# A linear attention's normaliser, as four column-grouped row products and one turning matmul per head

## The chip, the cores and the metric

The program runs on one NeuronCore of a Trainium2 chip. The metric is the device time of one execution in microseconds. The five engines that matter are TensorE (PE, whose weight loads appear apart as PEld), VectorE (DVE), ScalarE (ACT), GpSimd (POOL) and the DMA queues that SyncE (SP) issues. Each executes its own instructions in the order in which they were written, and they meet only through semaphores.

## The reference, cut to what matters

The program computes two layers. The change lies in the second layer's attention, which has 16 query heads of 128 channels, 4 key and value heads, 4 batches of 512 tokens and no softmax. For each batch:

```python
sq, sk = elu(q) + 1, elu(k) + 1                 # q: 16 heads, k: 4 heads, each [512, 128]
kv    = einsum('bhsd,bhse->bhde', sk, v)
qkv   = einsum('bhsd,bhde->bhse', sq, kv)
k_sum = sk.sum(axis=2)
norm  = einsum('bhsd,bhd->bhs', sq, k_sum)      # the normaliser: one number per token and head
attn  = qkv / (norm[..., None] + 1e-6)
out   = attn @ Wo.T                             # heads side by side, 2048 channels to 512
```

The kernel folds the last product into the heads: for head h it makes M = kv @ Wo_h (128 x 512), then sq_h @ M, scaled row by row by 1/norm and added into one accumulator `acc`.

## The kernel before, in words

The program is a sequence of stages: `front`, `recurrence_and_gate`, `linear_attention`, `relu_gate`. Only `linear_attention` changes. It works batch by batch (b = 0 to 3; the first has a few extra steps for loading and splitting the weights). In a batch TensorE turns the normalised input (`xT`), projects k and v for four tiles of 128 tokens each, makes `kvT` and `ksum`, and then goes through the 16 heads. All of its work is a list of jobs, `jobs`, which is the order in which TensorE issues them. `Ring` hands each job the next of the 8 PSUM banks, so job number i may start only when the reader of job i - 8 has finished (`ring.vacated`).

In the part with the heads the list reads, for each h: `q h`, `M h`, `norm h-1`, `head h-1` for the four token tiles. Head h's query product thus runs ahead of head h-1's output products. What each job is on TensorE:

- `q h`: 12 products of 128x512, the three-term split of an exact float32 product into pairs of fp32r (function `product3`, lines 579 to 581), four input tiles deep.
- `M h`: one float32 product of 128x512 (L1725). The trace has two records for each float32 product.
- `norm h`: four float32 products (L1730), one per token tile. The stationary operand is a tile of `sq` (128x128), the moving operand one column, the key sum `ksum`. The result is 128 tokens x 1 for each tile, which is the shape VectorE needs: tokens on partitions.
- `head h, t`: three products of 128x512, one of the four output tiles.

What surrounds the heads on the other engines, per head and in this order:

- ScalarE: `reluq` (relu of q, L1660), `expq` (exp of VectorE's min, L1664), the high part of M (`M_part[0]`, L1669). Ahead of `expq` it waits for VectorE's min of the same head, and VectorE waits for `reluq`.
- VectorE: min(q, 0) (L1571), in some heads a step of the next batch's layer norm (L1517 to L1532), then norm + 1e-6 (L1582) and its reciprocal (L1587), four accumulations into `acc` (L1598), the low part of M (L1606), and `sq` split into its two parts (L1611, L1613).
- GpSimd: `sq` = `expq` + `reluq` (L1495).

Of the kernel before, what the change touches and what calls it, by code (L numbers as in the profile page):

```python
# [14 lines left out]
P = 128  # L15
B = 4
T = 512
TT = T // P
# [1275 lines left out]
def linear_attention(nc, w, x1, spill, relay, handed, hand):  # L1294
# [11 lines left out]
    for h in range(QH + 1):  # L1306
        if h < QH:
            jobs += [("q", h), ("M", h)]
        if h > 0:
            jobs += [("norm", h - 1)] + [("head", h - 1, t) for t in range(TT)]  # L1310

    with ExitStack() as ctx:
# [25 lines left out]
        kvT = sb("kvT", [P, KVH, D])  # L1338
        ksum = sb("ksum", [P, KVH])
        expq = [sb(f"expq{i}", [P, T]) for i in range(2)]  # L1340
# [39 lines left out]
        sq_hi_ready = signal("sq_hi_ready", QH)  # L1380
        sq_lo_ready = signal("sq_lo_ready", QH)
        norm_ready = signal("norm_ready", QH)
        inv_ready = signal("inv_ready", QH)
# [10 lines left out]
        for h in range(QH):  # L1394

            reader["q", h] = (minq_ready, h + 1)
            reader["M", h] = (M_lo_ready, h + 1)
            reader["norm", h] = (norm_ready, h + 1)
            for t in range(TT):
                reader["head", h, t] = (acc_ready, h * TT + t + 1)  # L1400
# [64 lines left out]
        def _(pool):  # L1465
# [16 lines left out]
            def sequence(b, first, last):  # L1482
                for h in range(QH):
                    if first and h + AHEAD < QH:
                        low(h + AHEAD)
                    if h == (LN_HEAD if first else RSQRT_HEAD) and not last:
# [5 lines left out]

                    pool.wait_ge(*(ring.product(("norm", h - 2), b) if h >= 2 else
                                   ring.product_before(("norm", QH - 2 + h), b)))
                    nc.gpsimd.tensor_tensor(sq[h % 2][:, :], expq[h % 2][:, :], reluq[h % 2][:, :],  # L1495
# [129 lines left out]
        def _(act):  # L1625
            for s in (xT_ready, expk_ready, kvT_ready, ksum_ready, reluq_ready, expq_ready, M_hi_ready):
                s.ahead(act)

            def high(h):
# [5 lines left out]
            def sequence(b, first):  # L1635
# [14 lines left out]
                act.wait_ge(*ring.product(("ksum", 0), b))  # L1650
                nc.scalar.activation(ksum[:, :], ring.place(("ksum", 0))[:, 0:KVH], ACT.Copy).then_inc(ksum_ready.sem, 1)

                act.wait_ge(w_loaded, 3 * 16)
                act.wait_ge(*sk_ready.now(b, TT))
                for h in range(QH):
                    if first and h + AHEAD < QH:
# [6 lines left out]
                    act.wait_ge(*minq_ready.now(b, h + 1))  # L1663
                    nc.scalar.activation(expq[h % 2][:, :], expq[h % 2][:, :], ACT.Exp).then_inc(expq_ready.sem, 1)  # L1664
                    act.wait_ge(*ring.product(("M", h), b))

                    act.wait_ge(*(ring.product(("head", h - 2, TT - 1), b) if h >= 2 else
                                  ring.product_before(("head", QH - 2 + h, TT - 1), b)))
                    nc.scalar.activation(M_part[h % 2][0][:, :], ring.place(("M", h))[:, :],  # L1669
                                         ACT.Copy).then_inc(M_hi_ready.sem, 1)  # L1670

            sequence(0, True)
# [4 lines left out]
        def _(pe):  # L1677
# [4 lines left out]
            def sequence(b, first):  # L1682
                for job in jobs:
# [37 lines left out]
                    elif kind == "M":  # L1721
# [3 lines left out]
                        last = nc.tensor.matmul(place[:, :], kvT[:, n // GROUPS, :], Wo[:, n, :], start=True, stop=True)  # L1725
                    elif kind == "norm":
                        pe.wait_ge(*sq_ready.now(b, n + 1))
                        pe.wait_ge(*ksum_ready.now(b, 1))
                        for t in range(TT):
                            last = nc.tensor.matmul(place[:, t:t + 1], sq[n % 2][:, t * P:(t + 1) * P],  # L1730
                                                    ksum[:, n // GROUPS:n // GROUPS + 1], start=True, stop=True)
                    else:
                        t = job[2]
                        pe.wait_ge(*M_lo_ready.now(b, n + 1))
                        pe.wait_ge(*sq_lo_ready.now(b, n + 1))
                        last = product3(nc, place[:, :], [q[:, t * P:(t + 1) * P] for q in sq_part[n % 2]],
                                        [q[:, :] for q in M_part[n % 2]], True, True)
# [533 lines left out]
```

## Time and profile before

| | us |
|---|---|
| median of 3 runs | 1979.46 (1970.95 to 1991.2) |
| profiled execution | 1981.94 |
| its span, first to last instruction | 1980.1 |
| TensorE busy in it | 1805.2 (91%), mean granted clock 0.953 |
| VectorE busy | 1204.3 (61%) |
| ScalarE busy | 369.7 (19%) |
| GpSimd busy | 549.2 (28%) |
| span of the stage `linear_attention`, about | 890 to 1540 |

A profile comes from one execution. Its rows give a start in us from the first instruction, a duration, the engine, the line of the kernel, the operation, what it writes and reads, and how often. The durations of matmuls are modelled ends over measured starts: matmuls overlap, so that the distance between two starts, not the duration, is what one costs TensorE. A granted clock of 1.00 is 2.4 GHz, 0.50 is 1.2 GHz.

### The profile page before, as it was taken

The numbers are of one execution on the slowest core, as the hardware profiler recorded it, in microseconds if no ns is written. First come the engines' busy times: TensorE is split into PE (matmuls) and PEld (weight loads), VectorE is DVE, ScalarE is ACT, GpSimd is POOL, SyncE is SP. The second block draws the span as 40 slices with busy tenths as digits, with TensorE's granted clock in tenths as the row PEclk, the third lists the DMA queues.
The fourth block names the chain that finished last, engine by engine and source line by source line (L and its number), as shares of the span: only waits on it lengthen the run. The fifth ranks groups of instructions, "written<-read, shape, count | busy, mean of one in ns | idle before, by whom it ended". The sixth has DMA issues, their size and how long they took to land. (4 is left out here: it accounts for less than half of the span.)

```text
span 1980.1 us, 22000 instructions
## 1 busy us (share of the span) xinstructions
PE 1805.2 (91%) x6900; PEld 1187.2 (60%) x6900; DVE 1204.3 (61%) x1821; ACT 369.7 (19%) x621; POOL 549.2 (28%) x419
## 2 busy tenths in 40 slices
PE   7898894898998989939998999999999699999997
PEld 3333333655646647416775876777677356788885
DVE  4776784676877768633775686577477554523333
ACT  1212221011011111102331222122122221211111
POOL 3443442344553554331320121111011232101001
PEclk9999996898999989968999999999999799999998
DMA  4423328663675745403101001001100221302010
GB/s 188 180 96 133 140 102 272 220 220 116 199 223 180 223 162 199 142 33 144 38 33 64 1 1 64 0 0 51 55 0 0 75 74 32 139 1 85 5 58 32
DMA packets 81236, 197.06 MB, mean 100 GB/s; under 512 B 6352, under 2 KB 28752, under 8 KB 72592
## 3 DMA queue, kind: packets, MB, share of 16 engines
q1 hardware_dynamic: 81168, 196.27, 29.1%
q8 instruction: 28, 0.46, 0.1%
q14 instruction: 40, 0.33, 0.1%
HBM read 152.21 MB, written 44.04 MB: 99 GB/s over the span
## 5 line engine op out<-in xcount | busy, mean ns | idle before, releaser
L846 POOL TENSOR_TENSOR r_rS<-r_S,r_rT 128x512 f32<-128x512 f32 x128 | 182.9, 1430 | 259.4 <-DVE r_S L935 259.4
L1495 POOL TENSOR_TENSOR l_sq<-l_expq,l_reluq 128x512 f32<-128x512 f32 x64 | 83.1, 1299 | 474.9 <-ACT l_expq L1664 474.9
L1598 DVE SCALAR_TENSOR_TENSOR l_acc<-l_ps,l_inv,l_acc 128x512 f32<-128x512 f32 x240 | 167.0, 749 | 29.6 <-PE l_ps L581 29.6
L579 PE MATMUL r_ps<-relay_part,r_w_part 128*128 128x512 f32 x352 | 149.5, 425 | 21.9 <-DMA r_w_part<-scratch_wgu 13.5
L935 DVE TENSOR_TENSOR_SCAN r_S<-r_dT,r_ps 128x512 f32<-128x512 f32 x128 | 156.3, 1221 | 11.4 <-POOL r_rS L846 7.1
L1265 PE MATMUL r_ps<-Wdn,r_h 128*128 128x512 f32 x352 | 154.9, 596 | 0.0
L1991 DVE CAST g_x_part<-g_x 128x512 fp32r<-128x512 f32 x64 | 37.6, 587 | 187.6 <-ACT g_x L2049 187.6
L581 PE MATMUL r_ps<-relay_part,r_w_part 128*128 128x512 f32 x352 | 142.4, 405 | 0.0
L580 PE MATMUL r_ps<-relay_part,r_w_part 128*128 128x512 f32 x352 | 142.2, 404 | 0.0
L1265 PEld LDWEIGHTS r_ps<-Wdn,r_h 128*128 128x128 f32 x352 | 65.6, 190 | 86.6 <-issue 86.6
L579 PE MATMUL l_ps<-l_M_part,l_sq_part 128*128 128x512 f32 x256 | 107.4, 420 | 8.0 <-DVE l_sq_part L1613 8.0
L1698 PE MATMUL l_ps<-relay,l_xT 128*128 128x512 f32 x256 | 111.1, 594 | 0.0
L1571 DVE TENSOR_SCALAR l_expq<-l_ps,l_bq 128x512 f32<-128x512 f32 x64 | 48.0, 750 | 97.4 <-ACT l_reluq L1660 97.4
L579 PE MATMUL l_ps<-l_x_part,l_Wq 128*128 128x512 f32 x256 | 106.4, 416 | 0.0
L579 PE MATMUL g_ps<-g_x_part,g_Wup 128*128 128x512 f32 x256 | 104.2, 407 | 1.6 <-DVE g_x_part L1979 1.6
L581 PE MATMUL l_ps<-l_x_part,l_Wq 128*128 128x512 f32 x256 | 104.4, 408 | 0.0
L579 PE MATMUL g_ps<-g_Wdn,g_x_part 128*128 128x512 f32 x256 | 104.2, 407 | 0.0
L580 PE MATMUL l_ps<-l_x_part,l_Wq 128*128 128x512 f32 x256 | 104.0, 406 | 0.0
L581 PE MATMUL g_ps<-g_x_part,g_Wup 128*128 128x512 f32 x256 | 102.7, 401 | 0.0
L580 PE MATMUL g_ps<-g_x_part,g_Wup 128*128 128x512 f32 x256 | 102.6, 401 | 0.0
L580 PE MATMUL l_ps<-l_M_part,l_sq_part 128*128 128x512 f32 x256 | 101.8, 398 | 0.0
L581 PE MATMUL l_ps<-l_M_part,l_sq_part 128*128 128x512 f32 x256 | 101.4, 396 | 0.0
(184 smaller groups left out, 3422.3 us busy)
## 6 DMA issues: line engine op xcount, KB each, us to landing
r_w_part<-scratch_wgu SPq DMA_DIRECT2D x44, 1024.0 KB, 5.2
r_V<-scratch_v SPq DMA_DIRECT2D x96, 256.0 KB
scratch_wgu<-f_halves SPq DMA_DIRECT2D x32, 384.0 KB, 3.6
relay<-scratch_x SPq DMA_DIRECT2D x12, 1024.0 KB, 6.7
relay<-scratch_v SPq DMA_DIRECT2D x32, 256.0 KB
relay<-in_x SPq DMA_DIRECT2D x4, 1024.0 KB, 9.0
scratch_x<-f_xT SPq DMA_DIRECT2D x4, 1024.0 KB, 8.7
r_xs<-in_x SPq DMA_DIRECT2D x4, 1024.0 KB, 6.8
```

Of the source, the lines that this page charges most:

```text
L579: nc.tensor.matmul(out, left[1], right[0], start=start, stop=False)
L580: nc.tensor.matmul(out, left[0], right[1], start=False, stop=False)
L581: return nc.tensor.matmul(out, left[0], right[0], start=False, stop=stop)
L846: nc.gpsimd.tensor_tensor(rS[u % RS][:, :], S[u % 2][:, 0:T], rT[u // DK][:, :], ALU.mult).then_inc(rS_ready.sem, 1)
L935: nc.vector.tensor_tensor_scan(S[u % 2][:, 1:T + 1], dT[hh][:, :], kv, 0.0, ALU.mult, ALU.add).then_inc(S_ready.sem, 1)
L1265: last = nc.tensor.matmul(place[0][:, :], h[:, j, n * P:(n + 1) * P], Wdn[:, j, :], start=(j == 0), stop=(j == JT - 1))
L1495: nc.gpsimd.tensor_tensor(sq[h % 2][:, :], expq[h % 2][:, :], reluq[h % 2][:, :], ALU.add).then_inc(sq_ready.sem, 1)
L1571: nc.vector.tensor_scalar(expq[h % 2][:, :], ring.place(("q", h))[:, :], bq[:, h:h + 1], 0.0, ALU.add, ALU.min).then_inc(minq_ready.sem, 1)
L1598: last = nc.vector.scalar_tensor_tensor(acc[:, t, :], ps, inv[g % 2][:, t:t + 1], acc[:, t, :], ALU.mult, ALU.add)
L1698: last = nc.tensor.matmul(place[:, :], xT[:, kt, n * P:(n + 1) * P], Wkv[kind][:, kt, :], start=(kt == 0), stop=(kt == KT - 1))
L1991: nc.vector.tensor_copy(hi[:, :], x2[j % 2][:, :]).then_inc(x2_hi_ready.sem, 1)
```

## The change

Per head the job `norm` is split in two. The new job `rows` multiplies the other way round: the stationary operand is `ksum`, copied out to 32 equal columns, and the moving operand is a 128-token tile of `sq` (128x128). Each of the four tiles goes to its own group of 32 columns of the array, so its result lands on 32 partitions of the bank, and the four together fill 128 partitions x 128: 32 equal rows for each token tile. ScalarE copies this block to SBUF (`copy_rows`, tile `norm_rows`), and the new job `norm` is one float32 product with `norm_rows` stationary and four columns of the identity moving, which gives the 128 tokens x 4 that VectorE read before. VectorE's work is unchanged.

The job list becomes, for each h: `q h`, `rows h-1`, `M h`, `head h-1, 0`, `norm h-1`, `head h-1, 1` to `3`. It is 8 jobs per head, where it was 7. On ScalarE `copy_rows(h-1)` stands behind `expq` of head h and ahead of the high part of M. `ksum` grows from 128x4 to 128x4x32, written by the same ScalarE instruction, once per batch.

```diff
--- before.py
+++ after.py
@@ -1305,9 +1305,13 @@
             + [("kvT", 0), ("ksum", 0)])
     for h in range(QH + 1):
         if h < QH:
-            jobs += [("q", h), ("M", h)]
+            jobs += [("q", h)]
         if h > 0:
-            jobs += [("norm", h - 1)] + [("head", h - 1, t) for t in range(TT)]
+            jobs += [("rows", h - 1)]
+        if h < QH:
+            jobs += [("M", h)]
+        if h > 0:
+            jobs += [("head", h - 1, 0), ("norm", h - 1)] + [("head", h - 1, t) for t in range(1, TT)]
 
     with ExitStack() as ctx:
         def sb(name, shape, dt=F32):
@@ -1336,7 +1340,8 @@
         sk = sb("sk", [P, TT, KVH * D])
         v = sb("v", [P, TT, KVH * D])
         kvT = sb("kvT", [P, KVH, D])
-        ksum = sb("ksum", [P, KVH])
+        ksum = sb("ksum", [P, KVH, P // TT])
+        norm_rows = [sb(f"norm_rows{i}", [P, P]) for i in range(2)]
         expq = [sb(f"expq{i}", [P, T]) for i in range(2)]
         reluq = [sb(f"reluq{i}", [P, T]) for i in range(2)]
         biased, expk = reluq, expq
@@ -1379,6 +1384,7 @@
         x_lo_ready = signal("x_lo_ready", KT)
         sq_hi_ready = signal("sq_hi_ready", QH)
         sq_lo_ready = signal("sq_lo_ready", QH)
+        rows_ready = signal("rows_ready", QH)
         norm_ready = signal("norm_ready", QH)
         inv_ready = signal("inv_ready", QH)
         acc_ready = signal("acc_ready", QH * TT)
@@ -1395,6 +1401,7 @@
 
             reader["q", h] = (minq_ready, h + 1)
             reader["M", h] = (M_lo_ready, h + 1)
+            reader["rows", h] = (rows_ready, h + 1)
             reader["norm", h] = (norm_ready, h + 1)
             for t in range(TT):
                 reader["head", h, t] = (acc_ready, h * TT + t + 1)
@@ -1490,8 +1497,8 @@
 
                     pool.wait_ge(*(sq_lo_ready.now(b, h - 1) if h >= 2 else sq_lo_ready.before(b, QH - 1 + h)))
 
-                    pool.wait_ge(*(ring.product(("norm", h - 2), b) if h >= 2 else
-                                   ring.product_before(("norm", QH - 2 + h), b)))
+                    pool.wait_ge(*(ring.product(("rows", h - 2), b) if h >= 2 else
+                                   ring.product_before(("rows", QH - 2 + h), b)))
                     nc.gpsimd.tensor_tensor(sq[h % 2][:, :], expq[h % 2][:, :], reluq[h % 2][:, :],
                                             ALU.add).then_inc(sq_ready.sem, 1)
 
@@ -1623,8 +1630,15 @@
 
         @block.scalar
         def _(act):
-            for s in (xT_ready, expk_ready, kvT_ready, ksum_ready, reluq_ready, expq_ready, M_hi_ready):
+            for s in (xT_ready, expk_ready, kvT_ready, ksum_ready, reluq_ready, expq_ready, rows_ready, M_hi_ready):
                 s.ahead(act)
+
+            def copy_rows(b, h):
+                act.wait_ge(*ring.product(("rows", h), b))
+                act.wait_ge(*(ring.product(("norm", h - 2), b) if h >= 2 else
+                              ring.product_before(("norm", QH - 2 + h), b)))
+                nc.scalar.activation(norm_rows[h % 2][:, :], ring.place(("rows", h))[:, 0:P],
+                                     ACT.Copy).then_inc(rows_ready.sem, 1)
 
             def high(h):
                 cols = slice(h * D, (h + 1) * D)
@@ -1648,7 +1662,8 @@
                 act.wait_ge(*ring.product(("kvT", 0), b))
                 nc.scalar.activation(flat(kvT[:, :, :]), ring.place(("kvT", 0))[:, :], ACT.Copy).then_inc(kvT_ready.sem, 1)
                 act.wait_ge(*ring.product(("ksum", 0), b))
-                nc.scalar.activation(ksum[:, :], ring.place(("ksum", 0))[:, 0:KVH], ACT.Copy).then_inc(ksum_ready.sem, 1)
+                nc.scalar.activation(ksum[:, :, :], ring.place(("ksum", 0))[:, 0:KVH].unsqueeze(2).broadcast_to(
+                    [P, KVH, P // TT]), ACT.Copy).then_inc(ksum_ready.sem, 1)
 
                 act.wait_ge(w_loaded, 3 * 16)
                 act.wait_ge(*sk_ready.now(b, TT))
@@ -1662,12 +1677,15 @@
 
                     act.wait_ge(*minq_ready.now(b, h + 1))
                     nc.scalar.activation(expq[h % 2][:, :], expq[h % 2][:, :], ACT.Exp).then_inc(expq_ready.sem, 1)
+                    if h > 0:
+                        copy_rows(b, h - 1)
                     act.wait_ge(*ring.product(("M", h), b))
 
                     act.wait_ge(*(ring.product(("head", h - 2, TT - 1), b) if h >= 2 else
                                   ring.product_before(("head", QH - 2 + h, TT - 1), b)))
                     nc.scalar.activation(M_part[h % 2][0][:, :], ring.place(("M", h))[:, :],
                                          ACT.Copy).then_inc(M_hi_ready.sem, 1)
+                copy_rows(b, QH - 1)
 
             sequence(0, True)
             with act.Fori(1, B) as b:
@@ -1723,12 +1741,17 @@
                         if first and n == 0:
                             pe.wait_ge(wo_loaded, 16)
                         last = nc.tensor.matmul(place[:, :], kvT[:, n // GROUPS, :], Wo[:, n, :], start=True, stop=True)
-                    elif kind == "norm":
+                    elif kind == "rows":
                         pe.wait_ge(*sq_ready.now(b, n + 1))
                         pe.wait_ge(*ksum_ready.now(b, 1))
+                        width = P // TT
                         for t in range(TT):
-                            last = nc.tensor.matmul(place[:, t:t + 1], sq[n % 2][:, t * P:(t + 1) * P],
-                                                    ksum[:, n // GROUPS:n // GROUPS + 1], start=True, stop=True)
+                            last = nc.tensor.matmul(place[t * width:(t + 1) * width, 0:P], ksum[:, n // GROUPS, :],
+                                                    sq[n % 2][:, t * P:(t + 1) * P], start=True, stop=True)
+                    elif kind == "norm":
+                        pe.wait_ge(*rows_ready.now(b, n + 1))
+                        last = nc.tensor.matmul(place[:, 0:TT], norm_rows[n % 2][:, :], ident[:, 0:P:P // TT],
+                                                start=True, stop=True)
                     else:
                         t = job[2]
                         pe.wait_ge(*M_lo_ready.now(b, n + 1))
```

TensorE in the heads of a middle batch, before: the end of the job `q`, then `M` (L1725), `norm` (L1730), and the first of the next heads' tiles (`l_M_part`, `l_sq_part`); `l_ps5` and so on are the PSUM banks.

```order
L581 MATMUL l_ps5<-l_x_part0,l_Wq0 128x512
L1686 REGISTER_ALU
L1725 MATMUL l_ps6<-l_Wo,l_kvT 128x512
L1730 MATMUL l_ps7<-l_ksum,l_sq1 128x1 x4
L579 MATMUL l_ps0<-l_M_part01,l_sq_part11 128x512
L580 MATMUL l_ps0<-l_M_part11,l_sq_part01 128x512
L581 MATMUL l_ps0<-l_M_part01,l_sq_part01 128x512
L1686 REGISTER_ALU
L579 MATMUL l_ps1<-l_M_part01,l_sq_part11 128x512
```

The same place after the change:

```order
L581 MATMUL l_ps0<-l_x_part0,l_Wq0 128x512
L1749 MATMUL l_ps1<-l_sq1,l_ksum 32x128 x4
L1743 MATMUL l_ps2<-l_Wo,l_kvT 128x512
L1704 REGISTER_ALU
L579 MATMUL l_ps3<-l_M_part01,l_sq_part11 128x512
L580 MATMUL l_ps3<-l_M_part11,l_sq_part01 128x512
L581 MATMUL l_ps3<-l_M_part01,l_sq_part01 128x512
L1753 MATMUL l_ps4<-l_ident,l_norm_rows1 128x4
L1704 REGISTER_ALU
L579 MATMUL l_ps5<-l_M_part01,l_sq_part11 128x512
```

The four row products stand ahead of M, and the product that turns them stands between the head's first and second tile.

ScalarE over one head in the same place, before: relu, exp and the high part of M.

```order
L1660 ACTIVATE l_reluq1<-l_ps0,l_bq 128x512 [waits l_sq_ready,l_product]
L1663 REGISTER_ALU
L1664 ACTIVATE l_expq1<-l_expq1 128x512 [waits l_minq_ready]
L1665 REGISTER_ALU
L1667 REGISTER_ALU [waits l_product]
L1669 ACTIVATE l_M_part01<-l_ps1 128x512 [waits l_product]
```

And after:

```order
L1675 ACTIVATE l_reluq0<-l_ps0,l_bq 128x512 [waits l_sq_ready,l_product]
L1678 REGISTER_ALU
L1679 ACTIVATE l_expq0<-l_expq0 128x512 [waits l_minq_ready]
L1637 REGISTER_ALU
L1638 REGISTER_ALU [waits l_product]
L1640 ACTIVATE l_norm_rows1<-l_ps1 128x128 [waits l_product]
L1682 REGISTER_ALU
L1684 REGISTER_ALU [waits l_product]
L1686 ACTIVATE l_M_part00<-l_ps2 128x512 [waits l_product]
```

The copy of head h-1's rows (`l_norm_rows1`) stands behind the exp of head h (`l_expq0`), which itself waits for VectorE's min of head h (`l_minq_ready`).

## Rows read from the trace of the kernel before

**Rows 1.** Windows: us, busy time (count) by engine, PEclk, DMA share, GB/s.
```profile
488.00:600.00 112.00, 105.17 (x391) 60.88 (x390) 83.07 (x102) 16.09 (x30) 60.78 (x41) 0.99 0.65 207
...
1115.00:1220.00 105.00, 103.11 (x490) 82.20 (x489) 83.77 (x160) 24.80 (x43) 19.15 (x15) 1.00 0.00 1
```
**Rows 2.** Timeline, PE, one head: start us, us, engine, line, op, out<-in, count.
```profile
1201.62 0.39 PE L581 MATMUL l_ps<-l_x_part,l_Wq 128*128 128x512 f32 x1
1201.86 1.02 PE L1725 MATMUL l_ps<-l_Wo,l_kvT 128*128 128x512 f32 x2
1202.71 0.95 PE L1730 MATMUL l_ps<-l_ksum,l_sq 128*128 128x1 f32 x8
1203.52 0.48 PE L579 MATMUL l_ps<-l_M_part,l_sq_part 128*128 128x512 f32 x1
1203.84 0.40 PE L580 MATMUL l_ps<-l_M_part,l_sq_part 128*128 128x512 f32 x1
...
1206.36 0.40 PE L579 MATMUL l_ps<-l_x_part,l_Wq 128*128 128x512 f32 x1
...
1209.15 1.02 PE L1725 MATMUL l_ps<-l_Wo,l_kvT 128*128 128x512 f32 x2
```
**Rows 3.** Timeline of ACT over the same head; in brackets the idle time before.
```profile
1202.06 0.69 ACT L1660 ACTIVATE l_reluq<-l_ps,l_bq 128x512 f32<-128x512 f32 x1 [4.68 <-PE l_ps L581]
1203.56 0.63 ACT L1664 ACTIVATE l_expq<-l_expq 128x512 f32<-128x512 f32 x1 [0.82 <-DVE l_expq L1571]
1204.10 0.58 ACT L1669 ACTIVATE l_M_part<-l_ps 128x512 fp32r<-128x512 f32 x1
```
**Rows 4.** Timeline of DVE over the same head.
```profile
1202.78 0.75 DVE L1571 TENSOR_SCALAR l_expq<-l_ps,l_bq 128x512 f32<-128x512 f32 x1 [1.02 <-ACT l_reluq L1660]
...
1203.90 0.15 DVE L1582 TENSOR_SCALAR l_norm<-l_ps 128x4 f32<-128x4 f32 x1
1204.08 0.18 DVE L1587 RECIPROCAL l_inv<-l_norm 128x4 f32<-128x4 f32 x1
1204.59 2.81 DVE L1598 SCALAR_TENSOR_TENSOR l_acc<-l_ps,l_inv,l_acc 128x512 f32<-128x512 f32 x4 [0.32 <-PE l_ps L581]
...
1208.36 0.69 DVE L1613 TENSOR_TENSOR l_sq_part<-l_sq,l_sq_part 128x512 fp32r<-128x512 f32 x1
```
**Rows 5.** Lines of ACT by form: busy us, mean ns, idle before.
```profile
L1669 ACT ACTIVATE l_M_part<-l_ps 128x512 fp32r<-128x512 f32 x64 | 37.2, 581 | 0.0
...
L1651 ACT ACTIVATE l_ksum<-l_ps 128x4 f32<-128x4 f32 x4 | 0.7, 174 | 14.4 <-PE l_ps L1711 14.4
```
**Rows 6.** Timeline of PE around a column-grouped product in the recurrence stage.
```profile
490.77 0.40 PE L581 MATMUL r_ps<-relay_part,r_w_part 128*128 128x512 f32 x1
491.10 1.07 PE L1237 MATMUL r_ps<-r_rS,r_pick 128*32 128x512 f32 x8
492.10 1.09 PE L1182 MATMUL r_ps<-r_ident,r_o 128*128 128x128 f32 x8
493.38 0.50 PE L579 MATMUL r_ps<-relay_part,r_w_part 128*128 128x512 f32 x1 [0.19 <-DVE r_h L946]
```
**Rows 7.** Timeline of the weight loads (PEld) there.
```profile
491.10 0.16 PEld L1237 LDWEIGHTS r_ps<-r_rS,r_pick 128*32 128x32 f32 x8 [0.37 <-issue]
```
**Rows 8.** Timeline of PE at the end of batch 1.
```profile
1216.49 0.47 PE L579 MATMUL l_ps<-l_M_part,l_sq_part 128*128 128x512 f32 x1 [1.90 <-DVE l_sq_part L1613]
...
1219.30 1.91 PE L1690 MATMUL l_ps<-l_ident,relay 128*128 128x128 f32 x16
```
**Rows 9.** Timeline of DVE there.
```profile
1215.65 0.69 DVE L1613 TENSOR_TENSOR l_sq_part<-l_sq,l_sq_part 128x512 fp32r<-128x512 f32 x1
```
**Rows 10.** Timeline of PE near the end of batch 0.
```profile
1047.59 1.20 PE L1730 MATMUL l_ps<-l_ksum,l_sq 128*128 128x1 f32 x8 [4.06 <-DVE l_M_part L1606]
...
1049.31 0.63 PE L580 MATMUL l_ps<-l_M_part,l_sq_part 128*128 128x512 f32 x1
1049.73 0.63 PE L581 MATMUL l_ps<-l_M_part,l_sq_part 128*128 128x512 f32 x1
```

## The prediction, made before the changed kernel ran

> **What bounds the kernel now.** I read the page first (TensorE busy 91% of the span), then the windows, then one head in the timelines. In the middle of a batch of this stage TensorE is busy 103.11 of 105 us at a granted clock of 1.00, VectorE 83.77, ScalarE 24.80 [rows 1]. The timeline of TensorE shows a closed pattern: M starts at 1201.86 and again at 1209.15, so one head takes 7.29 us, and no row in between has idle time [rows 2]. TensorE alone sets the time there. The reader should see in the same rows what follows what: the last query product starts at 1201.62, M takes 0.85 (1201.86 to 1202.71), the normaliser 0.81 (to 1203.52), the head's twelve products run from 1203.52 to 1206.36, then the next query.
>
> ScalarE is idle for most of a head, but what it does comes in a fixed chain behind the query product [rows 3, 4]: relu at 1202.06, VectorE's min at 1202.78, exp at 1203.56, and the copy of M at 1204.10. The last starts 2.48 us after the last query product began. Today nobody on TensorE waits for the end of this chain in the same head. After the change somebody does, and this is what I cost below.
>
> **The change, part by part.**
>
> Removed: the four normaliser products, 0.81 us per head, and with them the slow start of the product behind them, whose second record comes 0.32 after the first, where 0.23 is usual [rows 2]: 0.09. Together 0.90.
>
> Added, the row products. This trace has the same form in the recurrence stage: four products of 32 columns each, two records each, 512 elements moving [rows 6]. The eight records hold TensorE from 491.10 to 492.10, 1.00 us. A single float32 product of 512 elements costs 0.85 [rows 2], 0.43 per record, so the four column groups run side by side: two record times, not eight. With 128 elements moving, each record time is a quarter, 0.11 in place of 0.43: 1.00 - 2 x 0.32 = 0.36. Entering costs 0.33 from start to start in place of 0.23 [rows 6], and the load of the weights stood idle for 0.37 ahead of it [rows 7]: 0.10 more. M behind it cannot have its weights loaded ahead either; the product at 493.38 with such a start took 0.50 in place of 0.40 [rows 6]: 0.10 more. Together 0.56.
>
> Added, the turning product: one of the four of today, 0.81 / 4 = 0.20, with the 0.09 behind it.
>
> If nobody waited, a head would change by -0.90 + 0.56 + 0.29 = -0.05 us, over 64 heads -3 us. That is not the forecast, because of the wait.
>
> Added, the wait. The turning product reads `norm_rows`, ScalarE writes that in `copy_rows(h-1)`, and this stands behind exp of head h. So it cannot start before the place where the copy of M starts now, 1204.10 in the head shown [rows 3]. Neither the row products nor their speed matters for it; they are done over a microsecond earlier. The copy is 128x128: between 0.174 us for 4 elements and 0.581 for 512 [rows 5], straight between them 0.27. Its release of TensorE I put at 0.10, between 0.03 (VectorE's min ends at 1203.53, exp starts at 1203.56 [rows 3, 4]) and 0.15 (the split ends at 1216.34 [rows 9], TensorE starts at 1216.49 [rows 8]). So the turning product starts at 1204.10 + 0.27 + 0.10 = 1204.47.
>
> When would TensorE be there? Row products at 1201.62 + 0.33 = 1201.95, M at 1202.31, the head's first tile at 1202.31 + 0.10 + 0.85 = 1203.26, three products of 0.23: 1203.95. It stands idle for 0.5 us in each head.
>
> From 1204.47 the path goes on: the turning product 0.20, its weights not loaded ahead 0.10, then nine products of the head, 0.32 + 8 x 0.23 = 2.16. The next query starts at 1206.93, today at 1206.36 [rows 2]: **+0.57 us per head**. It is a closed loop, query, relu, min, exp, copy, turn, three tiles, next query, so every head pays it.
>
> The Trainium skill (ScalarE: Activation LUTs, Rules for kernel authors) budgets about 0.3 us per activation plus 0.83 ns per element, an estimate of 0.41 for this copy. The rows do not agree: 0.581 for 512 elements, where it would give 0.72 [rows 5]. By the page the sum would be about 8 us higher.
>
> The same skill (TensorE: Matmul & The Clock Gate, Step-by-step: what each phase is for) says that the next weights load while the current matmul runs. Here the weights are what is waited for, and the row at 493.38 shows the load in the open after a wait [rows 6]. By the page alone, 0.10 less per head, the sum would be 6 us lower.
>
> Which heads pay: in each batch the turning products of heads 0 to 14 stand behind an exp, 15 x 4 = 60. One falls into the stall at the end of batch 0, where VectorE's layer norm holds TensorE for 4.06 us and the clock is at 1.2 GHz for some products behind it [rows 10]; I count nothing there. 59 x 0.57 = 33.6 us.
>
> The end of a batch: head 15 already waits for VectorE (1.90 us idle [rows 8]), with no query product to cover it. VectorE now reads the normaliser later: the turning product from 1204.47 and about 0.4 for its length and end, 1204.9, and another 0.4 for its two short operations, so the accumulation starts at about 1205.3 in place of 1204.59 [rows 4], 0.7 later. The last head starts that much later and has the turning product (0.29) within it, where today the normaliser lay in the idle time: +1.0 x 4 = 4 us.
>
> At nothing: VectorE's delay of 0.7 elsewhere. Its split of `sq` ends at 1209.05 [rows 4], and the next head's first product, which needs it, starts one period behind 1203.52 [rows 2], at 1210.81: 1.8 us of room. The copy of M comes 0.27 later; VectorE takes it up only behind four accumulations, over 3 us later [rows 3, 4]. The wider `ksum` is written once per batch, ahead of the query products. With eight jobs per head and eight banks each job waits for the reader of its own kind one head earlier, and all of these end before; the tightest is M's, whose reader has over 1 us. If VectorE's cover were gone, its delay would be added one for one.
>
> Sum: 33.6 + 4 = +37.6 us, on the profiled execution's 1981.94. That execution was 2.5 above the median of 1979.46, so against the median I say **2016 us**.
>
> Bounds: shortest of everything (copy 0.17, release 0.03, no open load) gives 1206.66, +0.30 per head and +20 us in all. Longest (copy as long as a full one, 0.58, release 0.15) gives 1207.29, +0.93 and +60. A copy of a quarter of the elements is nearer to 0.174 than to 0.581, so I take the straight line and the upper end is unlikely.
>
> **The rivals.**
>
> (a) The wait does not decide: the copy is there when TensorE arrives, at 1203.95. Then only TensorE's own sum counts, -3 us, about 1976. The point is 1204.47 against 1203.95: the chain would have to be 0.5 us shorter than rows 3 and 4 show. For it speaks that matmul ends are modelled; against it that starts are measured and ScalarE issues in order. A share of this case, with M also starting at once and the turning product almost free, would end faster by at most 0.2 x 64 = 13 us. 7%.
>
> (b) The clock: with 0.5 us of idle time in each 7.9, TensorE could fall to 1.2 GHz in parts. At the end of batch 0 it did behind 4.06 us of idle time, with starts 0.42 apart in place of 0.23 [rows 10]. Against it: in the recurrence stage TensorE was busy 105.17 of 112, 94%, at a clock of 0.99 [rows 1], and here it would be busy 94% too. If a tenth of the 470 us of heads ran at half the clock, +47 us more (64 x 7.3 / 10), 2063. 6%.
>
> (c) The column groups do not run side by side at 128 elements: eight records of 0.11 instead of two, +0.5 us. TensorE would arrive at 1204.45, still ahead of 1204.47. 2017: the same forecast; it changes what the profile shows, not the time. I put 10% on it, inside the forecast's share.
>
> (d) The chain is shorter by 0.2 to 0.4 us, by the lower bounds: 1990 to 2000. 10%.
>
> The forecast, (c) within it, has 77%.
>
> **Numbers.** The three runs of before spread over 20 us, so 1% (20 us) is about what can be told from no change. Faster by over 1%: part of (a), 2%. Within 1%: the rest of (a), 5%, and most of (d), 6%: 11%. Slower: 87%. The range from 1996 to 2034 leaves out (a), (b) and the lower edge of (d).
>
> **What would show it.** In the profile after: TensorE's turning product idle for about 0.5 us before it, released by ScalarE's copy, some 60 times; the copy at about 0.27 us, right behind exp; M starting every 7.86 us; the eight row records within 0.3 us of each other. The forecast is wrong if M comes every 7.3 us, if no idle time stands before the turning product, or if PEclk in these windows falls below 0.95.

## The result, and the profile after

| | before | after |
|---|---|---|
| median | 1978.28 us (4 runs) | 2012.88 us (4 runs, 2012.39 to 2015.07) |
| ratio to before | | 1.0164, 95% interval 1.0117 to 1.021 |
| profiled execution, its span | 1981.94, 1980.1 | 2015.07, 2013.2 |
| TensorE busy, granted clock | 1805.2 us (91%), 0.953 | 1813.4 us (90%), 0.953 |

The change made the kernel 1.6% slower, 34.6 us in the median and 33.1 between the two profiled executions. The prediction said 2016.

The timeline of TensorE over a head in the middle of the stage (start us, us, engine, line, operation), which answers to [rows 2]:

```profile
1209.87 0.70 PE L1743 MATMUL l_ps<-l_Wo,l_kvT 128*128 128x512 f32 x1
...
1217.02 0.39 PE L581 MATMUL l_ps<-l_x_part,l_Wq 128*128 128x512 f32 x1
...
1217.34 0.42 PE L1749 MATMUL l_ps<-l_sq,l_ksum 128*32 128x128 f32 x8
1217.69 1.13 PE L1743 MATMUL l_ps<-l_Wo,l_kvT 128*128 128x512 f32 x2
...
1218.88 0.39 PE L580 MATMUL l_ps<-l_M_part,l_sq_part 128*128 128x512 f32 x1
1219.11 0.40 PE L581 MATMUL l_ps<-l_M_part,l_sq_part 128*128 128x512 f32 x1
1219.89 0.36 PE L1753 MATMUL l_ps<-l_ident,l_norm_rows 128*128 128x4 f32 x2 [0.38 <-ACT l_norm_rows L1640]
1220.13 0.47 PE L579 MATMUL l_ps<-l_M_part,l_sq_part 128*128 128x512 f32 x1
```

M starts at 1209.87 and at 1217.69: a head takes 7.82 us, where it took 7.30. All four row products with their eight records stand between 1217.34 and 1217.69. Then comes the new hole. The head's third product starts at 1219.11, the next could start 0.23 later, at 1219.34, and the turning product (L1753) starts at 1219.89, 0.55 us later. The row gives the idle time as 0.38, since it counts from the modelled end of the product before, and it names who ended it: ScalarE's copy.

ScalarE over the same head, which answers to [rows 3]:

```profile
1217.44 0.69 ACT L1675 ACTIVATE l_reluq<-l_ps,l_bq 128x512 f32<-128x512 f32 x1 [5.03 <-PE l_ps L581]
1218.95 0.63 ACT L1679 ACTIVATE l_expq<-l_expq 128x512 f32<-128x512 f32 x1 [0.82 <-DVE l_expq L1578]
1219.49 0.26 ACT L1640 ACTIVATE l_norm_rows<-l_ps 128x128 f32<-128x128 f32 x1
1219.64 0.59 ACT L1686 ACTIVATE l_M_part<-l_ps 128x512 fp32r<-128x512 f32 x1
```

The copy starts where M's copy did, 2.47 us after the last query product's start (2.48 before), and ends at 1219.75. The row products that it reads had all begun before M did, at 1217.69. In the 0.82 us ahead of exp ScalarE had nothing to do.

The waits of the stage, in total, times and longest, tell the same for all heads:

```profile
PE l_ps L1753 <- ACT l_norm_rows L1640: 23.2, 59, 0.6
...
PE l_ps L579 <- DVE l_sq_part L1620: 10.9, 5, 2.6
```

59 heads wait for the copy, as counted beforehand. The second row is mostly the ends of the four batches. TensorE there, in batch 1, which answers to [rows 8]:

```profile
1225.40 0.50 PE L579 MATMUL l_ps<-l_M_part,l_sq_part 128*128 128x512 f32 x1 [2.61 <-DVE l_sq_part L1620]
...
1226.12 0.63 PE L581 MATMUL l_ps<-l_M_part,l_sq_part 128*128 128x512 f32 x1
1226.54 0.42 PE L1753 MATMUL l_ps<-l_ident,l_norm_rows 128*128 128x4 f32 x2
1226.82 0.77 PE L579 MATMUL l_ps<-l_M_part,l_sq_part 128*128 128x512 f32 x1
...
1227.82 0.63 PE L581 MATMUL l_ps<-l_M_part,l_sq_part 128*128 128x512 f32 x1
1228.25 0.63 PE L579 MATMUL l_ps<-l_M_part,l_sq_part 128*128 128x512 f32 x1
...
1230.05 1.91 PE L1708 MATMUL l_ps<-l_ident,relay 128*128 128x128 f32 x16
```

The last head starts 2.61 us of idle time late, and then its products follow each other at 0.43 us (1227.82 to 1228.25) where 0.23 is usual. The granted clock from 1226.10 to 1229.00 is 0.50, which is 1.2 GHz. Before, after 1.90 us of idle time, the twelve products took 2.81 us (1216.49 to 1219.30 [rows 8]) at a granted clock of 1.00; now they and the turning product take 4.65.

The window in the middle of the stage, which answers to [rows 1] (us, busy time by engine, PEclk, DMA share, GB/s):

```profile
1115.00:1220.00 105.00, 99.66 (x486) 67.84 (x484) 76.79 (x146) 27.37 (x56) 17.97 (x15) 1.00 0.00 1
```

TensorE lost 3.5 us of busy time in the window, and its clock stayed at 2.4 GHz.

### The profile page after: what moved, and what is told of

The parts are those of the page before. It is cut to its first block and busy times, and to the rows that moved or that the text cites. A ratio compares the mean times of both kernels' runs of the same rounds, so it can differ in the third digit from the quotient of the medians.

```text
span 2013.2 us, 22497 instructions
## 1 busy us (share of the span) xinstructions
PE 1813.4 (90%) x7028; PEld 1144.1 (57%) x7028; DVE 1204.4 (60%) x1821; ACT 381.0 (19%) x685; POOL 549.6 (27%) x419
## 5 line engine op out<-in xcount | busy, mean ns | idle before, releaser
L579 PE MATMUL l_ps<-l_M_part,l_sq_part 128*128 128x512 f32 x256 | 131.4, 513 | 10.9 <-DVE l_sq_part L1620 10.9
L579 PE MATMUL g_ps<-g_Wdn,g_x_part 128*128 128x512 f32 x256 | 104.7, 409 | 0.0
L581 PE MATMUL l_ps<-l_M_part,l_sq_part 128*128 128x512 f32 x256 | 103.5, 404 | 0.0
L580 PE MATMUL l_ps<-l_M_part,l_sq_part 128*128 128x512 f32 x256 | 102.8, 402 | 0.0
L581 PE MATMUL g_ps<-g_Wdn,g_x_part 128*128 128x512 f32 x256 | 102.1, 399 | 0.0
```

The lines of the kernel that those rows point to most:

```text
L579: nc.tensor.matmul(out, left[1], right[0], start=start, stop=False)
L580: nc.tensor.matmul(out, left[0], right[1], start=False, stop=False)
L581: return nc.tensor.matmul(out, left[0], right[0], start=False, stop=stop)
```

## Where the time went

For each kernel I took the starts of M from TensorE's timeline. "Heads" is the sum over the four batches from the first M to the sixteenth. "Ends" is the sum from the sixteenth M to the next batch's first product, so idle time at the turn of the loop over batches is in it; in the last batch it ends 0.23 us behind the start of the last head product. All are of the profiled executions. The first interval between two M's holds no head products (3.7 us before, 4.2 to 4.4 after), so that a batch has 14 full heads in "heads", and the output products of heads 14 and 15 are in "ends".

| kernel | a head | heads | ends | heads + ends |
|---|---|---|---|---|
| before | 7.30 | 424.2 | 49.0 | 473.2 |
| after | 7.82 | 461.3 | 49.6 | 510.9 |
| copy ahead of exp | 7.18 | 425.2 | 46.8 | 472.0 |
| rows twice | 7.82 | 462.2 | 47.1 | 509.3 |
| turn one tile later | 7.20 | 426.9 | 53.5 | 480.4 |
| copy behind M | 8.31 | 488.5 | 57.7 | 546.2 |
| copy ahead of exp, rows twice | 7.41 | 437.9 | 53.0 | 490.9 |
| copy ahead of exp, one column group | 7.83 | 462.0 | 46.1 | 508.1 |
| before, one product of four | 6.67 | 390.9 | 51.2 | 442.1 |
| copy ahead of exp, last turn first | 7.18 | 425.2 | 46.4 | 471.6 |
| the same, last split first | 7.18 | 425.3 | 42.7 | 468.0 |
| before, last split first | 7.30 | 424.2 | 40.5 | 464.7 |
| copy ahead of exp, last split first | 7.18 | 425.1 | 37.4 | 462.6 |

The stage's heads and ends grew by 37.7 us. The rest of the program, of which the change touches only the one `ksum` instruction per batch, was 4.6 us shorter in the profiled execution of after than of before.

The sums of "heads" hide a shift. In batch 0 the layer norm's stall lay behind the sixteenth M before (106.6 and 17.4 us) and lies ahead of it now (119.0 and 12.7), because with eight jobs per head M waits for the reader of the M before it. So batches 1 to 3 are the ones to compare: 105.9 became 114.2, and an end of 10.15 (1209.15 [rows 2] to 1219.30 [rows 8]) became 12.36 (1217.69 to 1230.05).

## The experiments

### The copy ahead of exp

```diff
                                          bias=bq[:, h:h + 1]).then_inc(reluq_ready.sem, 1)
+                    if h > 0:
+                        copy_rows(b, h - 1)
                     act.wait_ge(*minq_ready.now(b, h + 1))
                     nc.scalar.activation(expq[h % 2][:, :], ...Exp).then_inc(expq_ready.sem, 1)
-                    if h > 0:
-                        copy_rows(b, h - 1)
```

> The changed kernel with one move: on ScalarE the copy of head h-1's rows stands between relu and exp of head h, where ScalarE is idle for 0.82 us. Theory (the wait behind exp costs everything): the copy ends over a microsecond before TensorE reaches the turning product, the idle time of about 0.5 us before it goes, a head takes 7.25 us (7.82 less 0.55), and the time falls from 2013 to about 1977, within 5 us of the kernel before. Rival (the change costs by TensorE's own work: the switch to column groups and back, and one more product): nothing on TensorE changes, 2013 stays within 5.

Measured: 1977.68 us (12 runs), 0.999 of before, interval 0.997 to 1.0009. ScalarE and TensorE in one head:

```profile
1187.34 0.69 ACT L1675 ACTIVATE l_reluq<-l_ps,l_bq 128x512 f32<-128x512 f32 x1 [4.55 <-PE l_ps L581]
1187.92 0.27 ACT L1640 ACTIVATE l_norm_rows<-l_ps 128x128 f32<-128x128 f32 x1
1188.84 0.63 ACT L1681 ACTIVATE l_expq<-l_expq 128x512 f32<-128x512 f32 x1 [0.65 <-DVE l_expq L1578]
```

```profile
1187.59 1.13 PE L1743 MATMUL l_ps<-l_Wo,l_kvT 128*128 128x512 f32 x2
...
1189.01 0.40 PE L581 MATMUL l_ps<-l_M_part,l_sq_part 128*128 128x512 f32 x1
1189.24 0.28 PE L1753 MATMUL l_ps<-l_ident,l_norm_rows 128*128 128x4 f32 x2
1189.38 0.48 PE L579 MATMUL l_ps<-l_M_part,l_sq_part 128*128 128x512 f32 x1
...
1194.77 1.13 PE L1743 MATMUL l_ps<-l_Wo,l_kvT 128*128 128x512 f32 x2
```

The copy lies in what was idle time, the turning product follows 0.23 behind the product before it, and a head takes 7.18 us. Moving one ScalarE instruction by one place gives back 35 us, the whole of the loss. TensorE's own work, which is identical in both kernels, is thus not the cause. It is even 0.12 us per head cheaper than before. That does not reach the total, for heads and ends are only 1.2 us shorter than before: in batches 1 to 3 the heads fell from 317.6 to 314.7 us, and the ends grew from 31.7 to 34.9. TensorE at the end of batch 1 of this kernel:

```profile
1201.85 0.47 PE L579 MATMUL l_ps<-l_M_part,l_sq_part 128*128 128x512 f32 x1 [2.64 <-DVE l_sq_part L1620]
...
1203.88 0.63 PE L579 MATMUL l_ps<-l_M_part,l_sq_part 128*128 128x512 f32 x1
1204.30 0.63 PE L580 MATMUL l_ps<-l_M_part,l_sq_part 128*128 128x512 f32 x1
```

The last head waits for VectorE's split as before. TensorE merely comes there earlier and stands idle for 2.64 us instead of 1.90, and again products behind it are 0.42 apart.

### The row products twice

```diff
-                        for t in range(TT):
+                        for t in [*range(TT), *range(TT)]:
                             last = nc.tensor.matmul(place[t * width:(t + 1) * width, 0:P], ...
```

> The changed kernel with the four row products issued twice, the second time over the first. Theory: TensorE has 0.55 us of idle time ahead of the turning product, and the added work (eight more records, 0.2 to 0.36 us) fits in it: a head stays at 7.82, the time at 2013, at most 3 more. Rival (TensorE's own work sets the time): 60 x 0.2 to 0.36, 12 to 22 us more, 2025 to 2035.

Measured: 2015.05 us, 1.0181 of before (1.0153 to 1.021); after was 2012.88. A head takes 7.82 us as in the changed kernel, and its hole has shrunk:

```profile
1187.72 0.64 PE L1749 MATMUL l_ps<-l_sq,l_ksum 128*32 128x128 f32 x16
1188.29 1.13 PE L1743 MATMUL l_ps<-l_Wo,l_kvT 128*128 128x512 f32 x2
1190.27 0.36 PE L1753 MATMUL l_ps<-l_ident,l_norm_rows 128*128 128x4 f32 x2 [0.17 <-ACT l_norm_rows L1640]
```

The added 0.22 us (0.57 for the block instead of 0.35) came out of the idle time, 0.17 in place of 0.38. TensorE's work is off the path.

### The turning product one tile later

```diff
-            jobs += [("head", h - 1, 0), ("norm", h - 1)] + [("head", h - 1, t) for t in range(1, TT)]
+            jobs += ([("head", h - 1, 0), ("head", h - 1, 1), ("norm", h - 1)]
+                     + [("head", h - 1, t) for t in range(2, TT)])
```

> The changed kernel with the turning product one tile later in the job list, between the head's second and third tile. ScalarE's order is untouched. Theory: three more products (0.69 us) stand ahead of it, TensorE arrives 3.02 us after the start of the last query product where the rows are ready after 2.85, so the idle time goes and a head takes 7.25 to 7.35: about 1978. VectorE gets its normaliser 0.15 us later than in the changed kernel. Rival (TensorE's own work): 2013. If VectorE's later start mattered, it would be slower than 2013.

Measured: 1987.29 us (10 runs), 1.0043 of before (1.0019 to 1.0068). A head takes 7.20 us, as the theory has it: the wait is gone with ScalarE's order untouched. But the whole is 9 us slower than expected, and 10 slower than the kernel with the copy ahead of exp. The table shows where most of it is: the batch ends took 53.5 us instead of 46.8. TensorE at the end of batch 1:

```profile
1204.38 0.28 PE L1754 MATMUL l_ps<-l_ident,l_norm_rows 128*128 128x4 f32 x2
...
1209.81 0.77 PE L579 MATMUL l_ps<-l_M_part,l_sq_part 128*128 128x512 f32 x1 [3.33 <-DVE l_sq_part L1621]
```

The last head waits 3.33 us instead of 2.6. The turning product of head 14 starts 2.35 us behind M where it was 1.65 in the kernel with the copy ahead of exp, so VectorE gets the normaliser 0.7 us later, and at a batch's end nothing covers that. Four times 0.7 is 2.8 of the 6.7 us. The last head also starts at the low clock here: its first product lasts 0.77 us, 0.47 in the kernel with the copy ahead of exp.

### The copy behind the copy of M

```diff
-                    if h > 0:
-                        copy_rows(b, h - 1)
                     act.wait_ge(*ring.product(("M", h), b))
 ...
                     nc.scalar.activation(M_part[h % 2][0][:, :], ...Copy).then_inc(M_hi_ready.sem, 1)
+                    if h > 0:
+                        copy_rows(b, h - 1)
```

> The changed kernel with the copy of the rows one place later on ScalarE, behind the high part of M (about 0.5 us from start to start). Theory: the loop gets longer by all of it, 8.32 us per head in place of 7.82, 59 x 0.5 = 30 us more, 2043. Rival (TensorE's own work): no change, 2013.

Measured: 2056.96 us (2042.33 to 2059.2), 1.0373 of before (1.0333 to 1.0412). A head takes 8.31 us, 8.32 was expected, and heads and ends together are 35.3 us more than in the changed kernel. ScalarE and TensorE:

```profile
1207.52 0.58 ACT L1684 ACTIVATE l_M_part<-l_ps 128x512 fp32r<-128x512 f32 x1
1207.99 0.27 ACT L1640 ACTIVATE l_norm_rows<-l_ps 128x128 f32<-128x128 f32 x1
```

```profile
1208.40 0.35 PE L1753 MATMUL l_ps<-l_ident,l_norm_rows 128*128 128x4 f32 x2 [0.86 <-ACT l_norm_rows L1640]
```

Three places for one copy give 7.18, 7.82 and 8.31 us per head. From the second place to the third the copy starts about 0.47 us later, which is what M's copy ahead of it takes from start to start (1207.52 to 1207.99), and the head is 0.49 longer. In the first place nobody waits for it, and TensorE's own work sets the 7.18. The total is 44 us above after, 14 more than expected. Of these 5.3 are in heads and ends, in part the loop-end idle time told below; the rest lies outside them, and I did not settle it.

### The same doubling where nothing waits

The kernel with the copy ahead of exp, and the row products twice as above.

> The kernel with the copy between relu and exp, and the four row products issued twice. There the loop no longer has idle time, so the same added work that cost 2 us in the changed kernel should now be paid: theory: eight records more, 0.2 to 0.3 us per head on top of 7.18, 60 x 0.25 = 15 us, from 1978 to about 1993. Rival (small column-grouped products are hidden beside their neighbours whatever waits): 1978 stays.

Measured: 2000.91 us, 1.0105 of before (1.0065 to 1.0144). A head takes 7.41 instead of 7.18. The 0.23 that was free in the changed kernel is paid here in every head, 12.7 us over the heads. The ends took 6.2 us more, 2.6 of it idle time at the turns of the loop over batches, so the total is 23 above its base, not 15. Heads and ends account for 18.9 of the 23.

### All rows in one column group

```diff
-                            last = nc.tensor.matmul(place[t * width:(t + 1) * width, 0:P], ...
+                            last = nc.tensor.matmul(place[0:width, t * P:(t + 1) * P], ...
```

> The kernel with the copy between relu and exp, and all four row products written to the same 32 columns of the array, side by side along the bank (so the normaliser is made of other numbers; only the time is read). If the four column groups run side by side in the changed kernel, they cannot here: eight records of 0.11 in place of two, +0.5 us per head, 7.7, about 30 us more, 2008. If they did not run side by side anyway: 1978.

Measured: 2016.3 us, 1.0183 of before (1.0144 to 1.0222), 39 us above its base, 8 more than expected. The block of eight records:

```profile
1175.63 1.06 PE L1749 MATMUL l_ps<-l_sq,l_ksum 128*32 128x128 f32 x8
1176.62 0.70 PE L1743 MATMUL l_ps<-l_Wo,l_kvT 128*128 128x512 f32 x1
```

0.99 us from start to start, where the four groups take 0.35, and 7.83 us per head, 0.65 more; 60 times that is the 39. The column groups do run side by side at 128 elements; without it the change would lose 0.5 us per head against before even with the copy in the better place.

### One normaliser product of four, in the kernel before

```diff
-                        for t in range(TT):
+                        for t in range(1):
                             last = nc.tensor.matmul(place[:, t:t + 1], sq[n % 2][:, t * P:(t + 1) * P],
```

> The kernel before the change with one of its four normaliser products per head (the other three columns of the normaliser are left out; only the time is read). It measures what such a product costs TensorE in place: by the rows, 0.81 / 4 = 0.20 us each, three less are 0.61 per head, a head at 6.69 in place of 7.30, 60 x 0.61 = 37 us less, 1943. If the first of them carried most of the price (the weights that cannot be loaded ahead), less than 20 us would go: 1960 or more.

Measured: 1948.94 us, 0.9807 of before (0.9759 to 0.9855). A head takes 6.67 in place of 7.30: 0.21 per product, 0.20 was the term of the sum. Heads and ends are 31.1 us less, not 37. The heads gave 33.3, for an interval between two M's at the start of each batch hardly changed (7.25 in batches 1 and 2), and the ends grew by 2.2: the last head waits for VectorE there, so it started at nearly the same time behind M (7.15 us in batch 1, before 7.34), and in batch 1 seven of the eleven distances between its products were 0.42 or 0.43 us, where before all but the first were 0.22 or 0.23.

### The batch end

Three more kernels with the copy ahead of exp, and one without the change. First the turning product of head 15 ahead of that head's first tile:

```diff
-        if h > 0:
+        if 0 < h < QH:
             jobs += [("head", h - 1, 0), ("norm", h - 1)] + [("head", h - 1, t) for t in range(1, TT)]
+        if h == QH:
+            jobs += [("norm", h - 1)] + [("head", h - 1, t) for t in range(TT)]
```

> The kernel with the copy between relu and exp, and for the last head of a batch the turning product ahead of the head's first tile, so that it lies in the idle time in which TensorE waits for VectorE's split of head 15. Theory: 0.15 to 0.25 us per batch and VectorE's read of the normaliser a little earlier: 1 us in all, 1977. If the turning product at the end mattered more than by its own length: 1973.

Measured: 1978.09 us (12 runs), 0.9982 (0.996 to 1.0005): no difference from 1977.68 that these runs can tell.

Then, on top, VectorE's split of M and `sq` for head 15 ahead of the normaliser and accumulations of head 14 (`split(h)` is the block of L1606 to L1613):

```diff
+                    if h == QH - 1:
+                        split(h)
                     if h > 0:
                         g = h - 1
 ...
-                    if h < QH:
+                    if h < QH - 1:
+                        split(h)
```

> As the kernel before it, and on VectorE the split of M and of sq for head 15 ahead of the reading of the normaliser and the accumulations of head 14. Theory: the last head no longer waits for four accumulations and then the split, it starts about 6.4 us after the last query product's start in place of 7.9, TensorE's idle time there falls from 2.6 to about 1 us and the clock is not lowered behind it: 2 to 3 us per batch, 8 to 12 in all, 1967. Rival (the accumulations of head 14 only move the wait to the banks of head 15): 1977.

Measured: 1972.02 us (12 runs), 0.9949 of before (0.9926 to 0.9971), about half of the gain that was expected. The same move in the kernel before the change:

> The kernel before the change, with only VectorE's order at a batch's last head altered as in the kernel before this one: the split for head 15 ahead of the normaliser and accumulations of head 14. It tells how much of the 0.5% of that kernel comes from this move and how much from the change with its copy moved. Theory: all four batch ends lose the 1.9 us of TensorE's idle time; if TensorE then stands idle ahead of the next batch's first product as it did there (3.8 us, released by nothing that the profile shows), the gain is small, 0 to 4 us: 1976 to 1980, and the rest of the 0.5% is the change's. If the move alone gives all of it: 1971.

Measured: 1970.72 us (12 runs), 0.9948 (0.9925 to 0.9971). The forecast of 1976 to 1980 failed and the alternative, 1971, came: the loop's turns had no such idle time here. Its batch ends took 8.3 us instead of 10.15 in batches 1 and 2, and 40.5 in all instead of 49.0. So the move alone gives the 0.5%, and these runs show nothing that the change adds to it. What became of the change's 0.12 us per head is seen in TensorE at the end of batch 1 of the kernel with both:

```profile
1205.68 0.36 PE L1759 MATMUL l_ps<-l_ident,l_norm_rows 128*128 128x4 f32 x2 [0.57 <-ACT l_norm_rows L1646]
...
1208.51 0.39 PE L581 MATMUL l_ps<-l_M_part,l_sq_part 128*128 128x512 f32 x1
1212.68 1.54 PE L1714 MATMUL l_ps<-l_ident,relay 128*128 128x128 f32 x12 [3.78 <-issue]
```

There is 3.78 us of idle time that the profile puts down to no other engine ("issue"), at the turn of the loop over batches; its waits have it twice:

```profile
PE l_ps L1714 <- issue: 7.6, 2, 3.8
```

The last kernel leaves the turning product of head 15 behind its first tile, and is otherwise the same.

> The change with its copy between relu and exp, and VectorE's split of head 15 ahead of head 14's accumulations; the turning product of head 15 stays behind the head's first tile, so TensorE does not wait 0.57 us for its copy. Theory: heads at 7.18, batch ends at about 8 us, so that the kernel beats both the kernel before with the same reorder (1971, heads at 7.30) by 60 x 0.12 = 7 us, less 1 to 2 for the turning product at each end: about 1965. If TensorE again stands idle for 3.8 us at the loop's end in two batches, as in the kernel with the turning product first: 1972, and what that idle time is stays open.

Measured: 1972.01 us (12 runs), 0.9954 (0.9928 to 0.9979), not the 1965 of the theory. In its profiled execution heads and ends are 2.1 us shorter than in the kernel before with the same move, and the medians do not show it. The idle time at the loop's end is there in one of the two turns:

```profile
PE l_ps L1712 <- issue: 3.9, 1, 3.9
```

So three kernels beat both before and after, each 0.5% faster than before, and all three have the move on VectorE. The change with its copy in the right place neither adds to it nor takes from it within these intervals.

## Why the prediction was right

**The mechanism.** The step that mattered was that the turning product hangs on a copy behind exp. It was right: copy at 2.47 us after the last query product (2.48 said), 0.26 us long (0.27), turning product at 2.87 (1204.47 - 1201.62 = 2.85 said), idle 0.55 before it (0.5), 59 times. Moving the copy to either side, moving the turning product and doubling the row products each changed the time of a head as this says.

**The size per head.** 0.52 us, 0.57 said. The turning product in the open took 0.24 (1219.89 to 1220.13), not 0.30: I had put the whole exposed load on top of the price of a product, which already holds loads. The nine products behind it were right.

**TensorE's own sum.** The row block was 0.35 (0.36 said) and the four groups ran side by side, so rival (c) is out; shown, not argued, by the kernel with one group. I said -0.05 per head if nobody waited, and it is -0.12 (7.18 against 7.30): the turning product with its weights loaded ahead takes 0.14 (1189.24 to 1189.38), not a quarter of 0.81. So the sum for rival (a), -3, should have read about -7 (60 x 0.12). It was not seen in the time, because the batch ends took it back.

**The batch end.** The last head starts 0.8 us later counted from its last query product (1225.40 - 1217.02 = 8.38, before 1216.49 - 1208.92 = 7.57, where 1208.92 is 7.30 behind 1201.62), 0.7 said. But I had counted on full clock behind it. The head's products took 4.65 in place of 2.81: 0.28 for the turning product, nearly all the rest the low clock after 2.61 us of idle time. That is rival (b), not in the heads, where I had looked for it, but at the ends. With its 15 heads at 0.52 taken off, batch 1 grew by 2.8 us at its end instead of 1.0. Low-clock products are not the same in all batches, and the length of the idle time alone does not decide on them; the last section has the rows.

**The total.** +37.6 said for the stage, +37.7 measured; that they agree to 0.1 is luck, since two terms were off in opposite directions: less per head (59 x 0.52 = 31 in place of 33.6), more at the ends (7 in place of 4). By batch it is 7.8, 10.6, 10.5 and 8.9; the end of batch 3 had low-clock products before the change too (11.38 us, where batch 1 had 10.15). The profiled executions differ by 33.1, since the rest of the program happened to be 4.6 us shorter. The sum itself gives 2017 against the median (1979.46 + 37.6), not the 2016 that I wrote.

**The two prices from the Trainium skill.** The 0.3 us plus 0.83 ns per element (the Trainium skill, ScalarE: Activation LUTs, Rules for kernel authors) holds by that page for an activation whose bias is a 128x1 operand. The copy has none, so I should not have used it for the estimate of 0.41: the copy took 0.26, and M's copy, which has no such bias either, took 0.581 for 512 elements [rows 5]. The relu has one, `l_bq`, and took 0.69 for 512 [rows 3], where the page's figures make an estimate of 0.72.

That the next weights load while a matmul runs (the Trainium skill, TensorE: Matmul & The Clock Gate, Step-by-step: what each phase is for) does hold here once nobody waits for them. The turning product's weight loads in the changed kernel and in the kernel with the copy ahead of exp:

```profile
1219.86 0.30 PEld L1753 LDWEIGHTS l_ps<-l_ident,l_norm_rows 128*128 128x128 f32 x2 [0.79 <-issue]
```

```profile
1189.01 0.42 PEld L1753 LDWEIGHTS l_ps<-l_ident,l_norm_rows 128*128 128x128 f32 x2
```

In the first the load starts 0.03 us ahead of the product at 1219.89, behind the wait, and the product takes 0.24. In the second it starts 0.23 ahead of the product at 1189.24, together with the matmul before it, and the product takes 0.14.

## What to carry to other kernels

In these kernels ScalarE did its work in the order of the program, so whoever read the copy waited for everything that stood ahead of it. Before adding a hand-over to an engine that is mostly idle, ask not how long the new instruction is but what it stands behind, and put it where the engine waits anyway: here one place cost 0.64 us per head out of 7.82. When a move makes the main loop faster, look at the ends of the loop next, since a stage's idle time there absorbs work that is then paid again when it is moved out of it.

## What the runs showed of the hardware

- Four float32 products of 32 columns in four column groups, 128 elements moving, take 0.35 us from the start of the first to the start of the next product, and 0.99 in one group. The first of them starts 0.32 us behind the fp32r product before it (1217.02 to 1217.34) in place of 0.23; in the recurrence stage it was 0.33 [rows 6].
- A float32 product with 128x128 weights and few columns takes TensorE 0.21 us in a row of four (the kernel with one of four), 0.14 alone between fp32r products with its weights loaded ahead, 0.24 when its weights are what it waits for.
- TensorE's clock fell to 1.2 GHz in the last head of batch 1 of the changed kernel behind 2.61 us of idle time, and stayed at 2.4 GHz in its heads with 0.55 us of idle time in each 7.82 (PEclk 1.00 from 1115 to 1220).
- The length of the idle time alone does not decide it. In batch 3 of the kernel before, the last head starts behind 1.80 us of idle time, and its first products run at 0.50; in batch 2 of the kernel with the copy behind M it starts behind 2.62 us and runs at 1.00. The first product of each, and a window behind each (us, busy time by engine, PEclk, DMA share, GB/s):

```profile
1533.65 0.77 PE L579 MATMUL l_ps<-l_M_part,l_sq_part 128*128 128x512 f32 x1 [1.80 <-DVE l_sq_part L1613]
```

```profile
1534.10:1536.40 2.30, 2.30 (x7) 1.73 (x7) 0.75 (x1) 0.00 (x0) 0.00 (x0) 0.50 0.00 0
```

```profile
1423.28 0.47 PE L579 MATMUL l_ps<-l_M_part,l_sq_part 128*128 128x512 f32 x1 [2.62 <-DVE l_sq_part L1620]
```

```profile
1423.30:1426.50 3.20, 3.20 (x14) 2.35 (x14) 1.89 (x5) 0.00 (x0) 0.00 (x0) 1.00 0.08 10
```

- At the turn of the loop over batches TensorE sometimes stands idle for up to 3.9 us that the profile puts down to no other engine. In the trace its branch instruction there lasts 0.21 us in both turns of seven of the thirteen kernels (before and after among them) and 3.3 to 5.3 us in both turns of four. In the other two kernels it was short in one turn and about 5 us in the other, so the instructions alone do not decide it. What does is open. Up to 7.6 us of a program was such idle time.
